# A two-layer AdaLN transformer: single-instruction Gelu in the last two batches, a buffer of their own for the last down weights, and a new table of orders

## What is computed

```python
# layer 0, for every batch
h = layernorm(x) * (1 + ca) + sa;  x = x + ga * attention(h)          # 16 heads of width 8
h = layernorm(x) * (1 + cb) + sb;  x = x + gb * experts(h)            # silu(h w0) * (h w1), wo, top 2 of 8
# layer 1, for every batch
h = layernorm(x) * (1 + ca) + sa
n = layernorm(h) * ln_g + ln_b
v, gate = split(silu(n @ W_hidden + b_hidden))
qk = silu(n @ W_qk + b_qk);  q, k = qk * gamma + beta
x = x + ga * ((v * softmax(q.T k / S).sum(-1) * gate) @ W_out + b_out + h)
h = layernorm(x) * (1 + cb) + sb
x = x + gb * (gelu(h @ w1[b] + b1[b]) @ w2[b] + b2[b])                # gelu in its tanh form, 128 -> 512 -> 128
```

## Time and profile before

| | |
|---|---|
| median of 3 runs | 1074.13 us (1069.6 to 1074.72) |
| profiled execution | 1075.01 us, of which the span of instructions is 1072.8 us |
| granted TensorE clock, mean | 0.941 of full speed |
| PE (matmul) busy | 916.9 us, 85% of the span |
| DVE (VectorE) busy | 773.2 us, 72% |
| ACT (ScalarE) busy | 656.1 us, 61% |
| POOL (GpSimd) busy | 428.5 us, 40% |

### The profile page before, as it was taken

One profiled execution on the slowest core, in us unless ns is written; L12 is line 12 of the kernel. 1 busy time (PEld: TensorE's weight loads), 2 busy tenths in 40 slices (PEclk: granted clock), 3 DMA queues, 4 the chain that ended last, 5 costly groups with the idle time before them and its releaser, 6 DMA issues. The chain is left out here.

```text
span 1072.8 us, 15618 instructions
## 1 busy us (share of the span) xinstructions
PE 916.9 (85%) x5176; PEld 507.8 (47%) x5176; DVE 773.2 (72%) x1467; ACT 656.1 (61%) x1176; POOL 428.5 (40%) x537
## 2 busy tenths in 40 slices
PE   4147778998899899999998899999998899879876
PEld 2111134443454355654444655455565365558744
DVE  6565678768866877788768686888878766447675
ACT  2235564666666768667667576776856756755442
POOL 3241042325131826554324265662545525265310
PEclk9557899999999999999999999999999899979978
DMA  8510214001300040115000014032010010010001
GB/s 233 163 55 30 63 39 101 31 2 56 60 1 2 14 118 9 40 31 126 4 1 14 22 45 99 31 90 41 18 35 19 3 38 2 9 41 7 18 10 35
DMA packets 54536, 47.09 MB, mean 44 GB/s; under 512 B 12393, under 2 KB 50025, under 8 KB 53114
## 3 DMA queue, kind: packets, MB, share of 16 engines
q1 hardware_dynamic: 53898, 45.85, 16.8%
q10 hardware_dynamic: 560, 0.26, 0.1%
HBM read 30.97 MB, written 14.73 MB: 43 GB/s over the span
## 5 line engine op out<-in xcount | busy, mean ns | idle before, releaser
L1565 DVE TENSOR_REDUCE negmax<-scores_for_max 128x2 f32<-128x1024 f32 x252 | 307.6, 1221 | 67.9 <-PE scores_for_max L940 66.0
L1277 ACT ACTIVATE probs<-scores 128x1024 f32<-128x1024 f32 x256 | 262.4, 1025 | 114.9 <-PE scores L964 112.2
L974 PE MATMUL weighted_values<-probs,vaug 128*32 128x512 f32 x1024 | 143.2, 634 | 3.6 <-ACT probs L1277 3.6
L1038 PEld LDWEIGHTS shared_ab<-eo,mu 128*128 128x128 f32 x1024 | 128.6, 191 | 35.6 <-issue 25.2
L1038 PE MATMUL shared_ab<-eo,mu 128*128 128x128 f32 x1024 | 141.1, 281 | 3.7 <-ACT scaled L1391 2.0
L1963 POOL TENSOR_TENSOR acc<-acc,scaled 128x512 f32<-128x512 f32 x55 | 71.7, 1304 | 169.6 <-ACT scaled L1391 169.6
L572 PE MATMUL expert_units<-hb_hi,e_lo 128*128 128x512 f32 x224 | 111.9, 500 | 16.7 <-DVE mu L1706 9.8
L940 PE MATMUL scores_for_max<-ks,qs 48*128 48x512 bf16 x504 | 102.1, 402 | 26.5 <-DVE negmax L1565 22.3
L1700 DVE SCALAR_TENSOR_TENSOR mu<-th,expert_units 128x512 f32<-128x512 f32 x112 | 76.7, 685 | 66.1 <-ACT th L1319 65.6
L964 PE MATMUL scores<-qs,ks 51*128 51x512 bf16 x512 | 102.2, 396 | 25.4 <-ACT probs L1277 23.7
L1319 ACT ACTIVATE th<-expert_units 128x512 f32<-128x512 f32 x112 | 66.9, 597 | 83.0 <-PE expert_units L574 81.8
(11 more groups left out here) (320 smaller groups left out, 1591.5 us busy)
## 6 DMA issues: line engine op xcount, KB each, us to landing
parts_d<-parts SPq DMA_DIRECT2D x15, 384.0 KB, 2.5
qs<-parts_d SPq DMA_DIRECT2D x14, 384.0 KB, 6.1
ks<-parts_d SPq DMA_DIRECT2D x14, 384.0 KB, 9.3
w<-in_L_ffn_w SPq DMA_DIRECT2D x16, 256.0 KB, 3.8
parts_d<-parts SPq DMA_DIRECT2D x15, 256.0 KB, 2.7
xp<-in_L_attn_x SPq DMA_DIRECT2D x8, 256.0 KB, 2.9
probs<-in_L_ffn_w_kernel SPq DMA_DIRECT2D x2, 1024.0 KB, 7.9
x<-in_L_attn_x SPq DMA_DIRECT2D x8, 256.0 KB, 2.9
```

Source lines behind the costliest of these rows:

```text
L974: last = nc.tensor.matmul(pv[32 * j:32 * j + 32, :], vaug[:, kt, PAIRS * (j // 2) + GP * g + j % 2, :], probs[:, kt % 2, j % 2, j // 2, :] ...
L1038: last = nc.tensor.matmul(m0[:, at], mu[:, (2 * e + f) % 4, at], eo[:, e, f, :], start=(f == 0), stop=(f == HALVES - 1))
L1277: nc.scalar.activation(probs[:, kt % 2, j, :, :].rearrange("p m s -> p (m s)"), se[:, :], ACT.Exp)\
L1565: V.tensor_reduce(negmax[:, g % 2, :, n], max_bank(b, g, n)[:, :].rearrange("p (m s) -> p m s", m=2), AX, ALU.max, negate=True)\
```

## The change

Three things are done in code, and the table of orders is replaced.

1. For batches 6 and 7 the Gelu is one ScalarE instruction, `Gelu_apprx_tanh`, which reads the bank with b1 as its bias and writes the chunk for `dn`. `upa` and `upg` do nothing for these batches, the bias matmuls `upb` and the tile `b1row` are gone, and the factor 0.5 in `fin` becomes 1 (for batch 7 a plain add).
2. ScalarE holds the tables of one set of functions at a time. Before there is one table load in the program. Now there are four: the new helper `table` runs a one-column activation at three places so that the load falls there. Silu stays in its tanh form, and the tanh steps of batch 7 that stand between two of these places need no load of their own.
3. w2 of batch 7 goes into `qz`, a tile that is free once q and k of batch 6 are made (`w2_of`), so its load no longer waits for `dn` of batch 6.

```diff
+        switch = sb("switch", [P, 4])
...
+        def w2_of(b):
+            return qz[:, :, :].rearrange("p n c -> p (n c)").rearrange("p (c d) -> p c d", c=FCH) if b == LAST else w2[:, :, :]
...
             def c_loadd(b):
-                after_all(sp, ("c_w2g", b - 1, 1), ("c_keep3", b - 1, 1), ("c_dn", b - 1, 2))
+                after_all(sp, ("c_w2g", b - 1, 1), ("c_keep3", b - 1, 1))
+                if b == LAST:
+                    after_all(sp, ("c_vg", b - 1, 2), ("c_kq", b - 1, 2), ("c_kk", b - 1, 2))
+                else:
+                    after_all(sp, ("c_dn", b - 1, 2))
...
-            def upb(b, h):
-                if b == LAST:
-                    after(pe, "c_inu", b, 48)
-                    after(pe, "c_begun", 0, 2 + h)
-                    for c in range(2 * h, 2 * h + 2):
-                        after(pe, "c_hz", b, c + 1)
-                        last = nc.tensor.matmul(hid_bank[c], b1row[0:1, c * P:(c + 1) * P], ones[0:1, :], start=True,
-                                                stop=False)
...
+            def table(function, n):
+                nc.scalar.activation(switch[:, n:n + 1], nhalf[:, 0:1], function)
             def simexp(b):
+                if b == LAST:
+                    table(ACT.Exp, 1)
                 after(act, "c_nms", b, 1)
...
+                if b == LAST:
+                    table(ACT.Gelu_apprx_tanh, 2)
             def up(b, c):
+                if b == LAST - 1 and c == 0:
+                    table(ACT.Gelu_apprx_tanh, 3)
                 after(act, "c_up", b, c + 1)
-                if b == LAST:
-                    after(act, "c_vg", b, 2)
-                    nc.scalar.activation(spare[:, c, :], hid_bank[c], ACT.Square, scale=GELU_A ** 0.5)\
+                if b >= LAST - 1:
+                    if c == 0:
+                        after(act, "c_dn", b - 1, 2)
+                    got = hid_bank[c] if b == LAST else m1[:, :]
+                    nc.scalar.activation(gl[:, c, :], got, ACT.Gelu_apprx_tanh, bias=b1[:, c:c + 1])\
                         .then_inc(sig["c_u2"], 1)
                     return
...
             def upa(b, c):
+                if b >= LAST - 1:
+                    return
                 after(dve, "c_u2", b, c + 1)
-                if b == LAST:
-                    V.scalar_tensor_tensor(out=spare[:, c, :], in0=spare[:, c, :], scalar=1.0, in1=hid_bank[c], op0=ALU.add,
-                                           op1=ALU.mult).then_inc(sig["c_ub"], 1)
-                    return
...
-    ("P", "mod1"): dict(dve=(123, 194, 218, 222, 240, 244, 264, 298)),
+    ("P", "mod1"): dict(dve=(115, 251, 342, 354, 355, 416, 431, 449)),
```

More of the change, by code:

```diff
@@ new lines @@
+    ("C", "fin"): dict(dve=(515, 517, 644, 649, 735, 739, 809, 811, 882, 885, 938, 939, 1021, 1024, 1031, 1032)),
+    ("C", "outp"): dict(sp=(74, 94, 105, 114, 123, 129, 134, 136)),
+    ("C", "keep"): dict(pool=(81, 110, 147, 182, 214, 232, 258, 259), dve=(2, 4, 8, 10, 29, 80, 95, 1026)),
+    ("C", "keep3"): dict(pool=(112, 145, 176, 206, 226, 244, 265, 267), dve=(1, 5, 26, 35, 42, 103, 104, 1030)),
+    ("C", "w2g"): dict(pool=(77, 133, 169, 198, 212, 243, 261, 269)),
+    ("P", "e0hi"): dict(act=(12, 13, 15, 16, 18, 19, 49, 59)),
@@ new lines @@
+    ("B", "downd"): dict(dve=(27, 28, 33, 41, 44, 51, 52, 53, 63, 64, 67, 68, 73, 78, 1002, 1005)),
+    ("B", "gsum"): dict(dve=(30, 32, 45, 46, 49, 58, 62, 1003)),
+    ("C", "row"): dict(pe=(1, 2, 7, 10, 11, 13, 54, 1256)),
+    ("C", "upb"): dict(pe=(3, 4, 5, 6, 14, 16, 17, 18, 19, 23, 24, 26, 27, 29, 1337, 1340)),
+    ("C", "out0"): dict(pe=(8, 9, 12, 15, 20, 21, 22, 1334)),
+    ("P", "silu"): dict(act=(1, 2, 3, 4, 5, 6, 7, 8, 9, 10, 26, 27, 48, 56, 64, 75), dve=(61, 66, 70, 72, 74, 75, 76,
+        79, 81, 82, 85, 91, 200, 211, 215, 222)),
@@ L1153, in dn @@
                     for c in ((0, 1, 2), (3,))[h]:
-                        after(pe, "c_gl", b, c + 1)
+                        after(pe, "c_u2", b, c + 1)
                         for t in range(NT):
                             at = slice(t * P, (t + 1) * P)
-                            last = nc.tensor.matmul(dn_bank[t][:, at], gl[:, c, at], w2[:, c, :], start=(c == 0),
+                            last = nc.tensor.matmul(dn_bank[t][:, at], gl[:, c, at], w2_of(b)[:, c, :], start=(c == 0),
                                                     stop=(c == FCH - 1))
@@ L1166, in dn @@
                     for c in range(FCH):
-                        last = nc.tensor.matmul(m1[:, at], gl[:, c, at], w2[:, c, :], start=(c == 0),
+                        last = nc.tensor.matmul(m1[:, at], gl[:, c, at], w2_of(b)[:, c, :], start=(c == 0),
                                                 stop=(c == FCH - 1))
@@ L1176, in _ @@
                       ("C", "xT3"): c_xT3, ("C", "up"): up, ("C", "dn"): dn,
-                      ("C", "row"): row, ("C", "out0"): out0, ("C", "upb"): upb})
+                      ("C", "row"): row, ("C", "out0"): out0, ("C", "upb"): lambda b, h: None})
         @block.scalar
```

308 lines of the change are left out of this document (142 added, 166 removed), and 176 rows, old and new, of the table SLOTS.

## The result

The changed kernel is slower: a median of 1081.85 us (1077.59 to 1087.62, 8 runs) against 1074.1 (1066.47 to 1078.21, 8 runs), a ratio of 1.0093 with a 95% interval of 1.0064 to 1.0122. Measured once more, in another job, it was 1.0058 (1.0029 to 1.0086). The forecast was 1066.5, in a range of 1058.5 to 1077. The profiled execution has a span of 1079.2 us, 6.4 longer than before; the mean granted clock is 0.936 instead of 0.941. VectorE is busy 776.5 us instead of 773.2, although it has 16 instructions fewer.

The account below looks back on a forecast made before the run. TensorE (85% busy) was read as the bound, with the start and end timelines carrying the sum: -4.35 end, -3.5 start, 0 middle, -7.85 on 1075.0 giving 1067.2. The median, 0.9 lower, was rounded to 1066.5 us; range 1058.5 to 1077.

Parts of the forecast that it names:

- Gelu steps of VectorE and ScalarE in the chain: Batch 7's last chain: removing batch 6's Gelu steps saves 1.8 us on VectorE and 0.65 on ScalarE, together 2.45.
- w2g moved: End, GpSimd: w2g ahead of batch 7's powers shortens the last normalising, 1.1 us gained, with slack of 1.6 to 2.
- The exclusive port of the Trainium skill: End: GpSimd and VectorE lock a shared SBUF port, so moved w2g could cost 1.3 us; no chance given.
- Last Gelu: End, batch 7's experts: dn follows up without a hole, ending 3.6 us behind the last up; 0.8 gained.
- Table loads: End, ScalarE: three further table loads of 1.28 us each are hidden, so nothing is charged.
- The 2.7 us of the Trainium skill: End, ScalarE: a table load with its drain takes about 2.7 us, so the end gains 0.5 less; no chance given.
- The end in all: Batch 7's last chain and experts: terms of 2.45, 1.1 and 0.8 us give -4.35, bounds -5 and -1.
- The start up to the first exponential: Start: first maximum at 53.3 us, eighth ends 63.8, row of maxima ready 68.7, first exponential's product at 72.8, 4.2 earlier.
- Two fewer maxima are done by then, but ... they fit: Start: delayed maxima fit into the 1.12 us each exponential leaves idle, so -3.5 is kept; bounds -4.2 and +1.4.
- At 92% busy I take 0, with ±6: Middle, batches 1 to 6: TensorE is nearly full, so the new order changes nothing: 0 us, ±6.
- The slower rival: Middle: clock dips costing up to 5 us each at re-laid borders; two give 1076, three 1081; chance 0.10.

Follow-up runs that it names:

- code_only: New code with the order table of before; 1070.65 us, ratio 0.9981 to the kernel before; in a repeat 1068.62 us, 0.9959.
- old_to_b7: New code; old order up to what batch 7's first exponential needs, new order from there; 1072.4 us, ratio 1.0002 to the kernel before.
- new_in_b0: New code; new order only from batch 0's first exponential product to batch 1's first exponential, old order elsewhere; 1077.37 us, ratio 1.0045 to the kernel before.
- new_to_b1: New code; new order up to what batch 1's first exponential needs, old order behind; 1076.04 us, ratio 1.0040 to the kernel before.
- new_to_exp: New code; new order up to batch 0's first exponential product, then old; 1067.94 us, ratio 0.9962 to the kernel before; repeat 1067.32 us, 0.9957.
- old_to_b4: New code; old order up to what batch 4's first exponential needs, new order from there; 1074.04 us, ratio 0.9996 to the kernel before.
- order_new_gelu_old: Old code with the new order table, but the last chain's steps in the old order behind all else; 1086.87 us, ratio 1.0124 to the kernel before.
- old_to_b1: New code; old order up to what batch 1's first exponential needs, new order from there; 1083.62 us, ratio 1.0123 to the kernel before.
- old_to_end: New code; old order up to what batch 7's last down product needs, new order for the last chain; 1071.6 us, ratio 1.0001 to the kernel before.

## Why the prediction was wrong

Its sum was -4.35 for the end, -3.5 for the start and 0 for the middle. By the landmarks of the two profiles it came to -3.9 for the end, -0.3 up to the first exponential of batch 1 (-3.3 and then +3.0), and +10.6 from there to x2, +6.4 in all. The steps, one by one.

- **Gelu steps of VectorE and ScalarE in the chain: right.** 2.45 forecast, 2.53 measured up to xcn's step on ScalarE and up to the softmax, and 2.72 in code_only, where w2g is not in the way.
- **w2g moved: right as a step, little worth in the sum.** The normalising fell from 2.20 to 1.11. Its 1.1 is in the 3.62 at the first product of `up`, but at the last product only 2.99 are left (44.56 from x2 instead of 47.55), since the second half of `up` took 2.98 instead of 2.35. I had charged nothing for the clock there, with "1 to 2 us" as a bound; the measured price lies between nothing and the whole 1.1 from one execution to the next. And the slack that I gave w2g, 1.6 to 2, was not there: w2 landed 5.1 us after its issue (1023.21, by the wait of 3.54 before w2g), not 3.8, w2g ran from 1028.28, and the power began at 1030.06, just as it was wanted. It cost 0.19, by a 128x4 step of VectorE beside it that took 0.36 instead of 0.17; in the repeat it cost 0.45. From x2 to the end code_only needs 51.76 and its repeat 52.34, the changed kernel 51.70 and 51.65: nearly all of the end's gain is the new code's. The exclusive port of the Trainium skill ("SBUF — State Buffer", on the two sides of SBUF) holds there only for a VectorE step with two inputs in SBUF or in a two-port mode, which I had left out. The traces agree: beside GpSimd x2 took 1.75 against 0.69, `qt` 1.64 against 0.68 and the normalising 2.20 against 1.12, but the statistics steps, which read one tile, took 0.87 and 0.38 beside w2g, as elsewhere. So the 1.3 that this rival priced were lost only where w2 landed at the start of x2, in old_to_b7 (1.06).
- **Last Gelu: right.** `dn` ends 3.57 behind the last product, forecast 3.6.
- **Table loads: right.** Each took 1.28, and no step of batch 7 waited for one; the first held batch 6's first Gelu by 0.14 (product done at 1029.26, Gelu at 1029.44, where the later ones follow in 0.04). The 2.7 us of the Trainium skill ("ScalarE: Activation LUTs", "Terms") are not seen: with the one-column step behind it a load held ScalarE for 1.5 us. The cover of the first was thinner than I wrote: the granted clock was 0.61 from 1027.5 to 1040, and the last three of batch 6's four `up` steps took 2.0 to 2.1 instead of the first one's 1.1, so the last of its Gelus ended at 1038.56, 0.3 before ScalarE was wanted, where I had four microseconds.
- **The end in all:** 4.35 forecast, 3.92 measured.
- **The start up to the first exponential: right.** 53.3, 63.8 and 68.7 forecast, 53.21, 64.18 and 68.57 measured. The first exponential's product was forecast at 72.8, 4.2 earlier, and came at 73.74, 3.3 earlier.
- **"Two fewer maxima are done by then, but ... they fit", and with it that -3.5 of the start's gain stays: this step failed.** At the place that I had read the maxima do fit: the first four exponentials follow each other in 1.73 with the new order as with the old. What I put at 0.7 us is the rest of the new order between the first exponential and that of batch 1. It costs 0.64% in one pair (new_in_b0 less code_only, 1.0045 less 0.9981) and 0.78% in the other (new_to_b1 less new_to_exp), 7 to 8 us, and in both pairs the intervals are apart. That the new start without this part brings its gain is not shown: new_to_exp stands at 0.9962 and 0.9957, code_only at 0.9981 and 0.9959. The two maxima by themselves are free in the old order; if they cost something, it takes the new order around them. I had read one exponential's wait of 1.12 and not the list behind it.
- **"At 92% busy I take 0, with ±6" for the middle: wrong in value and in range, and the largest error of the sum.** Counting pairs of like steps on TensorE's list said nothing. From the first exponential of batch 1 to x2 the changed kernel took 10.6 us more (8.5 in its repeat). TensorE was idle 83.5 us there (82.4 in the repeat) instead of 74.3, and 71.7 and 75.0 in the two profiles of code_only. Batch 4, which takes 95.3 to 95.4 with the old order there, took 97.5 to 98.1 with the new one (96.2 in old_to_b4). VectorE needed 7.4 us more in the last 200 us (134.68 against 127.26). What I left out is that a new table changes which GpSimd step lies beside which VectorE step: VectorE has 16 instructions less, by my estimate some 11 us at 0.68, and is busy 3.3 us longer. That this lengthens the program is not shown, as said below.
- **The slower rival** (the clock falls in more places) had the right sign, 10%, and is part of it: between the first exponential of batch 7 and x2 the clock was 0.93 instead of 0.95. Of the 7.9 us by which this stretch is longer, 5.0 are idle time and 2.9 busy time, so it was not by itself the mechanism that I priced.

What stays open: which steps behind the first exponential cost the time. That the order does, and not the code, is shown (code_only and its repeat against the changed kernel and its repeat, and order_new_gelu_old). No run exchanges one engine's whole list in the middle, and the cuts by batch don't add up (old_to_b1 1.0123, old_to_b4 0.9996, old_to_b7 1.0002, and new_to_b1 to the changed kernel only half a per cent). The contention of VectorE and GpSimd is seen in the traces, but that it is the cause was not shown: moving one pair of steps back did not give the time back, and VectorE's longer busy time is also in old_to_b4, whose stretch is short.

For batch 0 the traces say a little more. Counted from its first exponential, the 28th comes at 54.6 in the changed kernel, 54.8 before and 50.6 in code_only. From there to the first one of batch 1 it is 10.6 before, in code_only, in new_to_exp and in the repeats of the two, 13.8 in the changed kernel and 12.9 in new_in_b0. So at the border to batch 1 the two orders differ by 2 to 3 us in every profile, and a part of that is the work moved over the landmark. Ahead of it they can't be told apart: the 28th exponential comes at 56.6 in new_to_exp, with the old order, and at 57.5 in new_in_b0, with the new one. An estimate from the windows agrees: the length less what the low clock takes (busy time by one minus the clock) is 56.2, 56.8 and 56.7 in before, code_only and new_to_exp, and 58.1 and 59.9 in the changed kernel and new_in_b0. In the changed kernel this is no waiting, since TensorE idles 17.2 us as before; in new_in_b0 it idles 20.3. How this makes 7 to 8 us in the median is not shown.

The lowest ratios are those of new_to_exp, the new code and the new start with the old order from the first exponential on: 0.9962 and 0.9957 of the kernel before, about 1067.5 us. The new code with the old order throughout can't be told apart from it.

## What to carry to other kernels

When a change brings new code and a new order of everything, price the order as a change of its own: put the new code into the old order first. A gain at the head of an in-order pipeline says nothing about the end until the stretch behind it has been looked at with the same care. And a step that waits for a transfer, moved ahead of a step that the chain needs, is worth what the landing time leaves of it: w2g's 1.1 us cost 0, 0.2, 0.45, 1.1 or 2.15 at its new place.

## What the runs showed of the hardware

The granted clock in the last block of products differs between executions of one kernel. The changed kernel's second four products of `up` took 2.98 us at a clock of 0.63 and, in its repeat, 1.88 at 1.00; those of code_only 2.02 and 2.58. In all of them TensorE had been idle for over 4.6 us before the transposes ahead of this block. A saving of 1.1 us before the block can be lost in one pair of profiles and kept in another.

Between code_only and its repeat, one and the same kernel, batch 0's attention took 61.2 us at a clock of 0.90 and 65.3 at 0.81, and yet their spans were 1067.9 and 1068.3: batches 1 to 6 and batch 7 differed by 2.9 and 1.8 the other way. Where a change is worth a few microseconds, one profile of each kernel can therefore point the wrong way.

An activation table load took 1.28 us at each of the four places, whatever set it loaded. The load of w2 for batch 7 (256 KB, behind two small transfers) let w2g start 3.9 us after its issue in old_to_end, 4.7 to 4.8 in four profiles, 5.1 in the changed kernel and 5.4 in its repeat; the median of such loads on the profile's page is 3.9.
